# Combining expert rows, the next token norm and query, key and value preparation in one block, by groups, with GpSimd adding

## The reference

```python
# layer 0, experts: two of eight for each token, weighted
gates = jnp.einsum('nk,nke->ne', topk_probs, onehot)
out = jnp.einsum('ne,nec->nc', gates, y)
t = t + out
# layer 1, attention: norm over a token's 64 channels, then
xn = (v - mean(v)) / sqrt(var(v) + 1e-6)
q = xn + xn @ Wq.T + bq        # k and v likewise
qn = q / max(norm(q over a head's 8 channels), 1e-12)   # k likewise
attn = scale * qn @ kn.T + bias;  out = softmax(attn) @ v
```

## Time and profile before

| | us |
|---|---|
| median of three runs | 1077.66 |
| profiled execution | 1081.72 |
| its span | 1079.9 |
| TensorE, VectorE, ScalarE, GpSimd busy in the span | 873.9, 706.0, 631.0, 303.5 |
| layer 0's experts, last scatter issued | 369.73 |
| rows landed, combination starts | 378.14 |
| norm's first instruction | 387.76 |
| first product of attention's first block | 406.39 |
| last turned group stored | 452.44 |
| first score product | 452.74 |

### The profile page before, as it was taken

One profiled execution on the slowest core, in us unless ns is written; L12 is line 12 of the kernel. 1 busy time (PEld: TensorE's weight loads), 2 busy tenths in 40 slices (PEclk: granted clock), 3 DMA queues, 4 the chain that ended last, 5 costly groups with the idle time before them and its releaser, 6 DMA issues. The chain is left out here.

```text
span 1079.9 us, 21175 instructions
## 1 busy us (share of the span) xinstructions
PE 873.9 (81%) x6842; PEld 586.4 (54%) x6842; DVE 706.0 (65%) x1796; ACT 631.0 (58%) x1289; POOL 303.5 (28%) x337
## 2 busy tenths in 40 slices
PE   4992498999999528498988848995868999958497
PEld 2772247999999518366666634443543444425232
DVE  7795746654444276688888867887685545445775
ACT  4662124654444246688888836885756777746353
POOL 3156107777777532300000020112230001025100
PEclk9896569999999855599999978998887999979699
DMA  4001703310100210011111000001000000000000
GB/s 132 2 1 39 133 16 99 95 36 20 26 22 19 69 36 18 22 51 39 58 39 58 30 20 1 2 1 34 27 1 2 0 0 0 1 22 1 2 1 39
DMA packets 25272, 32.71 MB, mean 30 GB/s; under 512 B 11582, under 2 KB 14665, under 8 KB 24814
## 3 DMA queue, kind: packets, MB, share of 16 engines
q1 hardware_dynamic: 20206, 27.50, 9.1%
q0 software_dynamic: 4992, 4.22, 1.6%
HBM read 19.31 MB, written 4.91 MB: 22 GB/s over the span
## 5 line engine op out<-in xcount | busy, mean ns | idle before, releaser
L1824 DVE SCALAR_TENSOR_TENSOR routed_hid_stage<-ps,routed_act_stage 128x512 f32<-128x512 f32 (+1 forms) x117 | 70.5, 603 | 98.4 <-ACT routed_act_stage L1601 97.1
L1601 ACT ACTIVATE routed_act_stage<-ps 128x512 f32<-128x512 f32 x117 | 69.9, 598 | 86.4 <-PE ps L1909 86.4
L1919 PE MATMUL ps<-w_sb,routed_hid_stage 128*128 x936 | 117.7, 269 | 0.0
L1152 ACT ACTIVATE hid_stage<-ps,b_col_sb 128x512 f32<-128x512 f32 x192 | 116.2, 696 | 0.3 <-PE ps L1103 0.2
L1909 PE MATMUL ps<-routed_x_stage,w_sb 128*128 128x256 f16 x858 | 113.5, 273 | 2.1 <-DVE routed_hid_stage L1824 1.2
L1919 PEld LDWEIGHTS ps<-w_sb,routed_hid_stage 128*128 128x128 f32 x936 | 113.6, 192 | 1.4
L412 POOL TENSOR_TENSOR st_sb<-st_sb,neg_half_sb 128x4 f32 (+1 forms) x32 | 37.5, 1173 | 250.8 <-DVE st_sb L407 250.8
L1657 POOL DMA_INDIRECT routed_got_stage<-expert_rows,take_stage x78 | 82.5, 1058 | 73.7 <-DVE give_stage L1795 50.1
L1103 PE MATMUL ps<-x_sb,w_sb 128*128 (+1 forms) x384 | 96.1, 395 | 3.5 <-ACT hid_stage L1152 3.5
L1117 PE MATMUL ps<-hid_stage,w_sb 128*64 128x512 f32 x384 | 93.9, 608 | 1.3 <-DVE gated_stage L1184 1.3
L1909 PEld LDWEIGHTS ps<-routed_x_stage,w_sb 128*128 x858 | 83.4, 103 | 10.6 <-issue 2.6
(11 more groups left out here) (395 smaller groups left out, 1872.2 us busy)
## 6 DMA issues: line engine op xcount, KB each, us to landing
w_stage_sb<-f_w SPq DMA_DIRECT2D x32, 176.0 KB
x_sb<-w_sb SPq DMA_DIRECT2D x16, 256.0 KB, 2.4
rt_sb<-vals_stage SPq DMA_DIRECT2D x16, 256.0 KB, 2.3
rel_bias_sb<-bias_bands SPq DMA_DIRECT2D x16, 128.0 KB
w_stage_sb<-f_w SPq DMA_DIRECT2D x14, 128.0 KB, 3.0
w_sb<-f_w SPq DMA_DIRECT2D x1, 1536.0 KB
routed_got_stage<-expert_rows,take_stage POOLq DMA_INDIRECT x78, 2.5
expert_out<-routed_rows_stage,give_stage POOLq DMA_INDIRECT x78, 2.2
```

What stands on the lines that cost most here:

```text
L1152: nc.scalar.activation(hid[:, n % RING, :], ps[:, n % BATCH, :], func, bias=b1_col[:, b:b + 1], scale=UNSCALE).then_inc(h_act, 1)
L1601: nc.scalar.activation(act_h[:, n, :], ps[:, H1 + (q + n) % 2, :], ACT.Silu, scale=UNSCALE).then_inc(h_act, 1)
L1824: last = nc.vector.scalar_tensor_tensor(hid[:, q % 2, n, 0:full], ps[:, H3 + (q + n) % 2, 0:full], UNSCALE, act_h[:, n, 0:full], ALU.mult, ...
L1919: last = nc.tensor.matmul(ps[:, Y + q % 2, h * C:(h + 1) * C], hid[:, q % 2, n, a * BLK + h * P:a * BLK + (h + 1) * P], w2[:, bass.ds(e * ...
```

## The change

The four row loads, ScalarE's scalings and VectorE's six instructions leave routed_experts, norm_stage's use before attention goes, and attention's first block does all three, by groups. Rows are read by SyncE in 16 transfers of four tiles, first rows to xn_tok, second rows to a part of sq or, from group 4 on, to a free part of w16; four semaphores count quarters. The gates move to a tensor that outlives the block. Per group, GpSimd multiplies the second row, VectorE the first (weight), and GpSimd makes both additions (combine). A new class GroupNormPlain, derived from GroupNormInPlace, squares over the spent second rows and is copied to xn_ch by ScalarE alone, from banks 6 and 7 in turn; the power takes 128x4 at a time. Turned queries and keys get banks 4 and 5 alone. The large memset goes from GpSimd to VectorE. Elsewhere two pairs of semaphores are merged: the selector's load in the first norm now counts on "f", which ScalarE waits for before copying it, and in the convolution of layer 3 one semaphore counts "cleared" and "weights ready".

```diff
-                    for h, s in enumerate(halves):
-                        for k, dst in enumerate((xn_tok, sq)):
-                            sp.dma_start(dst[:, s, :], slots_d.rearrange("(k p t) c -> k p t c", k=TOPK, t=NT)[k, :, s, :]
-                                         ).then_inc(y_loaded[h], 16)
...
-                    for h, s in enumerate(halves):
-                        act.wait_ge(y_loaded[h], 32)
-                        for t in range(s.start, s.stop):
-                            last = nc.scalar.activation(sq[:, t, :], sq[:, t, :], ACT.Copy, scale=gates[:, 1, t:t + 1])
-                        last.then_inc(rows_by_act, 1)
...
-                    for h, s in enumerate(halves):
-                        dve.wait_ge(y_loaded[h], 32)
-                        c.link(nc.vector.tensor_tensor(xn_tok[:, s, :], xn_tok[:, s, :], wide(gates[:, 0, s], C), ALU.mult))
-                        c.link(nc.vector.tensor_tensor(x_tok[:, s, :], x_tok[:, s, :], xn_tok[:, s, :], ALU.add))
-                        dve.wait_ge(rows_by_act, h + 1)
-                        c.link(nc.vector.tensor_tensor(x_tok[:, s, :], x_tok[:, s, :], sq[:, s, :], ALU.add))
...
-            norm_stage(1e-6, beside=Beside())
+            def second_rows(g):
+                half = GROUPS // 2
+                at_t = g % half * TPG
+                return sq[:, NT // 2 + at_t:NT // 2 + at_t + TPG, :] if g < half else late_rows[:, at_t:at_t + TPG, :]
...
+            token_norm = GroupNormPlain(1e-6, [6, 7] * (GROUPS // 2), second_rows)
+            TURNED = 4
...
                 def _(sp):
+                    load(sp, "l1", qkv_w[:, :], L1["qkv_w"])
+                    load(sp, "l1", proj_w[:, :], L1["proj_w"])
+                    load(sp, "l1", scale[:, :], L1["scale"].unsqueeze(0).broadcast_to((P, 2 * HEADS1)))
+                    for n in range(QUARTERS):
+                        for g in (2 * n, 2 * n + 1):
+                            for k, dst in enumerate((xn_tok[:, group_tiles(g), :], second_rows(g))):
+                                sp.dma_start(dst, by_slot[k, :, group_tiles(g), :]).then_inc(y_landed[n], 16)
+                    load_small(sp, F1)
...
                     def product(g):
+                        pe.wait_ge(g_copied, g + (token_norm.n0 + 1))
...
                     def turn(g):
                         pe.wait_ge(split, g + 1)
-                        if g >= 2:
-                            pe.wait_ge(t_copied, g - 1)
+                        if g >= 1:
+                            pe.wait_ge(t_copied, g)
...
-                    product(0)
-                    for g in range(GROUPS + 5):
-                        if g + 1 < GROUPS:
-                            product(g + 1)
-                        if g >= 5:
-                            turn(g - 5)
+                    pe.wait_ge(setup, IDENTITY_ADDED)
+                    for s in range(GROUPS + 6):
+                        if 0 <= s - 2 < GROUPS:
+                            product(s - 2)
+                        if 0 <= s - 6 < GROUPS:
+                            turn(s - 6)
+                        if 0 <= s - 1 < GROUPS:
+                            token_norm.turn(pe, s - 1)
...
+                    act.wait_ge(setup, SCALED)
+                    nc.scalar.activation(scale_h, scale_h, ACT.Exp).then_inc(rooted, 1)
+                    for s in range(GROUPS + 6):
+                        if 0 <= s - 2 < GROUPS:
+                            take_products(s - 2)
+                        if s < GROUPS:
+                            token_norm.square(act, s)
+                        if s >= 4 and s % 2 == 0 and s - 3 < GROUPS:
+                            root((s - 3) // 2)
+                        if 0 <= s - 1 < GROUPS:
+                            token_norm.copy(act, s - 1)
+                        if 0 <= s - 6 < GROUPS:
+                            take_turned(s - 6)
...
+                    def combine(g):
+                        xg, second = x_tok[:, group_tiles(g), :], second_rows(g)
+                        wait_landed(pool, g)
+                        c.link(nc.gpsimd.tensor_tensor(second, second, gate_wide(1, g), ALU.mult))
+                        pool.wait_ge(y_gated, g + 1)
+                        c.link(nc.gpsimd.tensor_tensor(xg, xg, xn_tok[:, group_tiles(g), :], ALU.add))
+                        nc.gpsimd.tensor_tensor(xg, xg, second, ALU.add).then_inc(summed, 1)
...
+                    for s in range(-1, GROUPS + 5):
+                        if 0 <= s - 1 < GROUPS:
+                            token_norm.power(pool, s - 1)
+                        if s + 1 < GROUPS:
+                            combine(s + 1)
+                        if 0 <= s - 5 < GROUPS:
+                            double(s - 5)
...
+                    nc.vector.memset(vals[:, :, :, VW:], 0.0)
...
+                    for s in range(-1, GROUPS + 5):
+                        if 0 <= s - 1 < GROUPS:
+                            token_norm.sum_squares(dve, s - 1)
+                            token_norm.variance(dve, s - 1)
+                        if 0 <= s < GROUPS:
+                            dve.wait_ge(summed, s + 1)
+                            token_norm.sum(dve, s)
+                            token_norm.centre(dve, s)
+                        if 0 <= s - 3 < GROUPS:
+                            sum_squares(s - 3)
+                            if s % 2 == 0:
+                                floor_pair((s - 3) // 2)
+                        if s + 1 < GROUPS:
+                            weight(s + 1)
+                        if 0 <= s - 1 < GROUPS:
+                            token_norm.scale(dve, s - 1)
+                        if 0 <= s - 5 < GROUPS:
+                            split_parts(s - 5)
+                        if s >= 4 and s % 2 == 0 and s - 3 < GROUPS:
+                            invert((s - 3) // 2)
```

More of the change, by code:

```diff
@@ L197, in metaformer, with norm_stage @@
         highs = [0]
-        def norm_stage(eps, stacked=False, prepare=None, beside=None):
+        def norm_stage(eps, stacked=False, prepare=None):
             hi0 = highs[0]
@@ L222, in _ @@
                         load(sp, "const", rank[:, :], wt_rank)
-                        sp.dma_start(sel32, selector_d).then_inc(sel_loaded, 16)
+                        load(sp, "f", sel32, selector_d)
                         load_small(sp, F0)
@@ L234, in _ @@
                         prepare_experts(prepare, sp=sp)
-                if beside is not None:
-                    @block.sync
-                    def _(sp):
-                        beside.sync(sp)
                 @block.vector
@@ L297, in _ @@
                         prepare_experts(prepare, act=act)
-                    if beside is not None:
-                        beside.scalar(act)
                     if stacked:
@@ L326, in _ @@
                         nc.gpsimd.memset(gate_parts[:, :, :], 0.0)
-                    if beside is not None:
-                        beside.gpsimd(pool)
                 @block.tensor
@@ L504, in low, with __init__, square, sum_squares @@
                                                x16[0:C, self.columns(g)], ALU.mult, ALU.subtract).then_inc(g_copied, 1)
+        class GroupNormPlain(GroupNormInPlace):
+            def __init__(self, eps, banks, squares):
+                GroupNorm.__init__(self, eps, False, banks[0])
+                self.banks, self.squares = banks, squares
+                self.prior = [max((h for h in range(g) if banks[h] == banks[g]), default=None) for g in range(GROUPS)]
+            def square(self, act, g):
+                act.wait_ge(g_centred, g + (self.n0 + 1))
+                nc.scalar.activation(self.squares(g), xn_tok[:, self.tiles(g), :],
+                                     ACT.Square).then_inc(g_squared, 1)
+            def sum_squares(self, dve, g):
+                dve.wait_ge(g_squared, g + (self.n0 + 1))
+                nc.vector.tensor_reduce(st[:, 1, self.tiles(g)], self.squares(g), AX.X,
+                                        ALU.add).then_inc(g_link, 2)
+            def copy(self, act, g):
+                act.wait_ge(g_turned, g + (self.n0 + 1))
+                nc.scalar.copy(xn_ch[0:C, self.columns(g)], self.turned(g)).then_inc(g_copied, 1)
         def linear_attention():
@@ L1454, in bias_bands @@
                      bands[:, :, SIDE - 1 - i:REL - i, :].rearrange("j h k l -> j h (k l)"))
+        QUARTERS = 4
+        y_landed = [sem(f"l1_y_landed{n}") for n in range(QUARTERS)]
+        top_gates = sb("top_gates", [P, TOPK, NT])
+        by_slot = slots_d.rearrange("(k p t) c -> k p t c", k=TOPK, t=NT)
         def routed_experts():
@@ L2102, in take_turned, with double @@
                         for b in range(2):
-                            last = nc.scalar.copy(qk_t[:, 2 * g + b, :], ps[:, 4 + 2 * (g % 2) + b, :].bitcast(F16))
+                            last = nc.scalar.copy(qk_t[:, 2 * g + b, :], ps[:, TURNED + b, :].bitcast(F16))
```

(30 more changed lines are left out.)

70 lines of the change are left out of this document (23 added, 47 removed).

## The result

The changed kernel takes 1092.18 us, median of four (1089.33 to 1095.33), against 1079.57 us (1077.41 to 1083.38) for the kernel before measured beside it: ratio 1.0114, 95% interval 1.0066 to 1.0161. It is slower by about one per cent, where no change was forecast. The profiled executions, 1090.23 and 1081.72 us, are 8.5 us apart; that is the difference which the traces can explain, and all that follows is about it. The medians are 12.6 us apart here and 10.2 us in `ctl_after`.

What follows compares the result with a forecast made beforehand. TensorE was taken to set the pace at first, then VectorE. The layout's end at 453.7, less 1.6, gave 452.1 against 452.4: -0.3 us, from a median of 1077.66 to 1077.3; range 1070 to 1086.

Steps and rivals of the forecast that it cites:

- The barrier (0.55 us): Start of attention's block: the boundary costs 0.55 us ahead of the row loads, first quarter asked for at 373.6.
- late landing: Row loads at the block's start: landing at 379.5 instead of 377.6 adds 1.6 us.
- The rest of the start: Attention's block up to TensorE's first product: listed steps and waits of 9.4 us, product at 387.0 instead of 406.4.
- The loop: First query/key/value products: each waits for ScalarE's channel copy, 5.1 us a group against 2.56 before.
- VectorE's stretch: From the first root at 403.3 to the last token scaling: 20.4 us work, 3.6 waits; last product at 430.8 to 433.3.
- the end: Last turns, with one bank pair: 4.1 us a group, last group stored at 453.7; with two pairs 450.8.
- The correction that was taken off: Sum for the third part: same layout gave 454.1 for 452.4 before, so 1.6 us came off, leaving 452.1.
- The port: VectorE and GpSimd holding each other up: about 0.33 us for each of eight steps, charged both ways, 2.6 us.
- no exclusion worth the name: Rival: GpSimd's additions fall into VectorE's one-input reductions, 2.6 us come off, 1074.7; chance 0.12.
- The rival in which GpSimd bounds: Additions of 1.4 to 1.7 us each make GpSimd pass VectorE: +14 us, 1092; chance 0.05, shared with other stalls.
- TensorE's higher clock: Rival: earlier start brings 2.4 GHz in query/key/value part, end 5 to 6 us forward, 1072; chance 0.15.
- The later blocks: Stream behind, 452.7 to the end: length unchanged; a change above 2 us would mean wrong in kind.

Runs made afterwards that it cites:

- ctl_after: The changed kernel, unaltered, measured and profiled again beside the kernel before: 1090.94 us, ratio 1.0091.
- Before_split: The kernel before with its combination (row loads, scalings, additions) moved unchanged into its own block; also cited as (1): 1086.55 us, ratio 1.0045.
- after_banks: The changed kernel with turned groups 5 and 7 put into banks 6 and 7: 1087.4 us, ratio 1.0052.
- dve_adds: The changed kernel with both additions issued by VectorE instead of GpSimd: 1090.24 us, ratio 1.0089.
- no_adds: The changed kernel without GpSimd's two additions, so layer 0's expert rows are left out of the result: 1083.62 us, ratio 1.0032.
- norm_only: The changed kernel with combination back in the experts' block, norm and preparation by groups, two bank pairs, ScalarE's memset, later small scale work: 1088.68 us, ratio 1.005.
- pool_memset: The changed kernel with the memset of 128x5888 moved from VectorE back to GpSimd: 1090.05 us, ratio 1.0074.
- experiment 3: The changed kernel with its 16 row loads at the experts' block's end, ScalarE's memset in four pieces, VectorE's first gate product earlier: 1089.41 us, ratio 1.0069.
- 5: The changed kernel with eight 256 KB row loads at the experts' block's end, ScalarE's memset, later small scale work, turns 5 and 7 in banks 6 and 7: 1086.66 us.
- ctl_before: The kernel before, unchanged, measured and profiled once more against its own twin: 1082.12 us, ratio 0.9991.

## Why the prediction was wrong

**The block boundary, the step that failed.** "The barrier (0.55 us)" was read from the earlier trace rows, where VectorE ended the block itself and everyone else had long been through. The new boundary stands right behind the last scatter, and there it costs GpSimd's drain: SyncE through at 371.5, open at 376.2. The loads were asked for at 377.45, not 373.6, landed at 381.72, not 377.6 or 379.5, and the first product came at 391.85, not 387.0: 4.9 us. No rival had it; the "late landing" was bounded at 1.9 us. Of these 4.9 us, 3.8 are the opening itself (376.24, where the prediction has 372.4), and the rest is the next point. Before_split shows the boundary alone (+4.7 us in the profile, +5.2 on the medians). The drain was in the trace of before, at L1552, for whoever asked what GpSimd did after 369.73.

**The rest of the start** was 1.0 us too short: opening to first product took 15.6 us, where the steps gave 387.0 less 371.9 + 0.5, that is 14.6. The durations were right (memset 4.96 for 5.0, pieces at 0.42, GpSimd's at 0.61, 0.72 and 1.04), the adding up was not. With the rows at 377.6 and VectorE free at 378.3 the wait is 0.7 us, not 0.2, and the terms listed for the first product make 9.8 us, not 9.4. Added up rightly they give a first gate product 5.9 us after the opening and the product of TensorE at 15.7. The trace has 6.8 (the memset began 1.3 us late) and then 8.8, together 15.6: an agreement by luck, of one part too short and one too long.

**The loop, VectorE's stretch and the end** were right but for the shift: products 5.2 us apart (5.1), then 6.8, 6.8, 6.1, 8.0 and 5.8 (mean 6.7 for "6 to 7"), the last at 435.85, which is 430.8 and 4.9, within 0.2 (with a turn ahead 433.3 was the other bound), the last turns 4.1 us apart as said, though only every other one waits for the banks, the last one stored at 458.0. VectorE was busy 35.7 of the 42 us from 403 to 445, so it idled for less than the fifth that would have spoken against the reading. Two pairs of banks were put at 2.9 us, after_banks measured 2.1.

**The correction that was taken off.** The steps, laid out raw, gave 453.7 for the end, and 1.6 us were taken off because the same layout was too long for the kernel before. With the start's 4.9 us the raw sum gives 458.6 and the corrected one 457.0; the trace has 458.0. The correction was no better than the raw sum: of its 1.6 us, 0.8 came from a turn at the higher clock, which this time ran at the lower one (1.86).

**The port.** The term was 2.6 us for both engines together, all eight powers charged. VectorE's busy time is 1.7 to 1.9 us longer for the additions (dve_adds, no_adds), so the term was of the right order. What was left out is the waiting: no_adds shows 4.1 us for all that the additions do, 2.1 of it ahead of the first product, where the prediction had 1.5. A gate product and a norm scaling of 0.42 took 0.67 and 0.83 beside GpSimd, a split of 0.69 took 1.21 and held GpSimd's addition for 0.3:

```profile
413.90 0.77 POOL L2135 TENSOR_TENSOR x_tok_sb<-x_tok_sb,xn_tok_sb 128x256 f32<-128x256 f32 x1 [0.42 <-DVE xn_tok_sb L2171]
414.01 1.21 DVE L2198 TENSOR_TENSOR w_stage_sb<-qk_stage,w_sb 128x512 f32<-128x512 f32 x1
...
414.75 1.05 POOL L2136 TENSOR_TENSOR x_tok_sb<-x_tok_sb,w_sb 128x256 f32<-128x256 f32 x1
```

So "no exclusion worth the name" is out for single instructions, small as the sum is, and GpSimd wasn't the bound either (additions at 0.72 to 1.05; from the first product to 438.6 it was busy 9.0 + 14.9 of 46.8 us). The rival in which GpSimd bounds named 1092 us, the measured number, but from additions of 1.4 to 1.7 us each: the number agrees by luck, the mechanism isn't there.

**TensorE's higher clock**, the first rival, was priced at 5 to 6 us. The clock of this stretch isn't a property of the kernel. The kernel before, profiled twice, had 0.51 in 407.6 to 417.6 and 0.96 in 409.6 to 419.6, with the same products running, and norm and preparation took 65.0 and 63.8 us. In the changed kernel two of the eight products ran at the higher clock (1.57 us, as at 435.85, instead of 2.93), and the stretch 403 to 445 had 0.62.

**The later blocks**, a second step that failed. The prediction put them at nothing, without a reason, and took a change of more than 2 us there for a sign that it is wrong in kind. They changed by 2.9: the similarity block lost 5.4 us of clock, the others gave 2.6 back. Nothing in one trace of before could have told it; it belongs in a range, about 4 us to either side (the 14 profiles have 623.4 to 630.3 us between the stream's start and the end).

**The number it was measured from.** The forecast of 1077.3 starts from the median of three runs, 1077.66. The medians of 22 to 26 runs beside the experiments are 1080.72 to 1081.35, at the level of the profiled execution. So 3 to 4 us of the distance between 1077.3 and 1092.18 lie in that small sample. Without them the measured time would still be outside 1070 to 1086.

**Where the expected gain went.** The change doesn't overlap what bounds. VectorE was the busiest engine (51.9 of 74.5 us) and idle mostly early; the written order lets it idle until the first root, and norm_only, in its one profile, shows the fusion alone ending behind the separate norm. That the order of the instructions is the reason is argued from the stretches; no run changed it. The prediction had this pace right and was neutral only since the lead of 19 us covered it; the lead was 14.5.

## What to carry to other kernels

A block boundary cost here what the slowest queue's drain cost, not what the last boundary in the trace shows: before moving work across one, list when each engine's queue is through with the block, GpSimd's above all when it has just issued scatters. An earlier start of one engine was worth nothing here until the engine that bounds the stretch could use it; ask in which microseconds that engine is idle, and whether its written order lets it fill them. And look at several later stages too: with a shift of some us TensorE's clock in a block 300 us further on changed, and its length by 5.4 us, as much as the change itself had cost (5.6).

## What the runs showed of the hardware

- GpSimd's DRAIN at the end of a block with indirect DMAs took 7930 to 8400 ns in the 14 profiles. In each it ended 5.9 to 6.0 us after the last scatter's issue had ended, and the next block opened 0.2 us later where nothing else held it up.
- A GpSimd memset, which reads nothing, stood in VectorE's way for the rest of its 5.00 us (2.19 us for 128x8 elements, in pool_memset).
- SyncE's issues of 128 KB (experiment 3), 256 KB (5) and 512 KB (1) alike came 0.47 us apart: their number, not their size, decided whether they fitted under the drain.
- TensorE stayed at 1.2 GHz (granted clock 0.50) through 391.85 to 409.05 though busy 11.4 of 17.2 us, and through the second 10 us of the similarity block though busy 9.5 of 10. The Trainium skill ("TensorE: Matmul & The Clock Gate", "Part 1: The HAM clock gate") has sustained work release the full clock; within those 10 us this trace doesn't show it.
- The clock that TensorE is granted for the same work differed between two executions of one kernel: 0.51 (kernel before, 407.6 to 417.6) and 0.96 (`ctl_before`, 409.6 to 419.6).
